# Two block tables and written-out instruction orders in a fused conv-attention, linear-attention and top-2 expert kernel

## The chip, the cores and the metric

One core of one Trainium2 chip runs the whole program. The metric is the device time in microseconds of one execution, the median of the runs. The profiled execution is one of them, with the profiler on.

## The reference

Eight images of 128 channels and 256 pixels go through three stages, each of which adds its result to its input. Tokens are (image, pixel) pairs, 2048 of them.

```python
# stage 1, conv attention, per image: softmax over the pixels of the same image
sim = einsum('bpm,bpn->bmn', q, k) / sqrt(64) + key_mask ; x = x + gamma * softmax(sim) @ v
# stage 2, linear attention over t = layernorm(tokens): the sequence is the image index (L = 8),
# the batch is the pixel, 8 heads of 16; causal: image i reads images j <= i
kv_cum = cumsum(k_ v^T) ; attn = (q_ . kv_cum) / max(q_ . k_cum, 1e-6) ; t = t + attn @ out_w.T + out_b
# stage 3, mixture of 8 experts, top 2 per token, over layernorm(t)
routing_weights, selected = top_k(softmax(x @ router_w), 2) ; renormalised to sum 1
out = sum_e combine[e] * ((silu(x @ w1[e]) * (x @ w3[e])) @ w2[e]) ; t = t + out
```

## The kernel before

**Attention stage.** Each image passes through conv attention (`conv_*`), linear attention (`lin_*`) and routing (`route_*`). The functions of one image are spread over later steps: `run_step(step, (stage, lag), ...)` calls, for each engine on its own, `stage(step - lag)` in the listed order. Engines are strictly in order and meet by semaphores. `lin_scores` (L652) makes, for image i, 2(i+1) products of a 128x128 weight (`qk`) with a moving operand of 8 columns; `lin_products` and `lin_values` are VectorE's large multiplications over i+1 images; `lin_out_turn` (L664) turns and sums on TensorE.

**Routing.** `route_top`, `route_index`, `route_mask`, `route_rank` and `route_slots` give each of a token's two choices a row in `rows_x` in memory: expert e owns the rows from e*CAP on, filled in order. `scatter` (L442, GpSimd, four indirect DMAs for each image) writes the normalised token, its weight and its destination there; `seen_done` counts the running totals per expert, `hm[:, .., 0, :]`.

**Table.** After image 7, TensorE sums the counts (L716), VectorE works out the first row and the expert of each of 39 blocks of 128 rows (L998 to L1014), TensorE turns the result (L718) and VectorE stores it as `table` (L1017). Engines read the table into registers with `table_reader`. `pad_lists` writes one block of empty rows behind each expert's list. SyncE waits for the table, the pads and all 32 scatters, then loads blocks (L395, `xb`, a ring of 12). TensorE runs 16 warm-up matmuls (L752).

**Expert stage.** For each of the 39 blocks: `turn_x` (L724), `gate_up` (L733, 4 f32 matmuls of 128x128, recorded as 8), ScalarE `silu` (L555), VectorE `hidden` (L1023), `down` (L742), VectorE `weigh` (L1040), and a scattered store to `rows_y` by GpSimd (L454). VectorE copies each block's gate and up weights from `W13` to `WB` (L1030), which is a ring of 3.

**End.** When every store has landed, SyncE loads both halves of `rows_y` in 6 parts (L404, L405), VectorE adds them to `t2` (L1058, L1060) and SyncE stores the result (L409).

Of the kernel before, what the change touches and what calls it, by code (L numbers as in the profile page):

```python
# [7 lines left out]
ALU = mybir.AluOpType  # L8
# [7 lines left out]
P = 128  # L16
B = 8
# [5 lines left out]
H = 8  # L23
# [10 lines left out]
BLOCKS = TOP_K * TOKENS // P + E - 1  # L34
ROW = P + 2
# [3 lines left out]
RING = 12  # L39
# [9 lines left out]
WARM_MATMULS = 16  # L49
SPLIT_FROM = 3  # L50
STEPS = B + 12
# [9 lines left out]
C_END = C_TURN_ROW + 1  # L61
# [8 lines left out]
def constants():  # L70
# [10 lines left out]
    f[:, C_TURN_ROW] = np.arange(P) * P  # L81

# [8 lines left out]
def hybrid_block(nc, x_ch, x_tok, w_conv, w_lin, w_router, w13, w2, vecs, bias_rows, cst_f, cst_tri, cst_dest,  # L91
                 out):
    ctx = ExitStack()
    with ctx:
# [15 lines left out]
        W13 = sb("W13", [P, E * 2 * F])  # L110
        W2 = sb("W2", [P, E * FK * P])
# [44 lines left out]
        num = sb("num", [P, 2, B, T * P])  # L156
        attT = sb("attT", [P, 2, N])
# [17 lines left out]
        cnt = sb("cnt", [P, E])  # L175
        pad_row = sb("pad_row", [1, E], I32)
        up = sb("up", [P, E], I32)
        nbi = sb("nbi", [P, E], I32)
        nblk = sb("nblk", [P, E])
        one8 = sb("one8", [P, E])  # L180
        ends = sb("ends", [P, E])
        past = sb("past", [BLOCKS, E])
        skipped = sb("skipped", [BLOCKS, E])
        exp_f = sb("exp_f", [BLOCKS, 1])
        first_f = sb("first_f", [BLOCKS, 1])
        rel_f = sb("rel_f", [BLOCKS, 1])
        row_f = sb("row_f", [BLOCKS, 1])
        steer = sb("steer", [BLOCKS, 2])
        table = sb("table", [2, BLOCKS], I32)
        pad = sb("pad", [P, ROW])  # L190
# [8 lines left out]
        y1 = sb("y1", [P, NT, P])  # L199
        y2 = sb("y2", [P, NT, P])  # L200
# [18 lines left out]
        ps_log = bank(BANK_LOG)[:, 0:T * E].rearrange("p (t e) -> p t e", t=T)  # L219
        ps_rank = bank(BANK_RANK)[:, 0:T * E].rearrange("p (t e) -> p t e", t=T)  # L220
        ps_cnt = bank(7)[:, N + 2 * T * E:N + 2 * T * E + E]

        ps_table = bank(7)[0:2, N + 2 * T * E + E:N + 2 * T * E + E + BLOCKS]
        ps_xbT = [bank(n)[:, 0:P] for n in BANKS_XBT]
        ps_yb = [bank(n)[:, 0:P] for n in BANKS_YB]
        ps_warm = bank(5)[:, 0:2 * P]
# [4 lines left out]
        ld_x = [sem(f"ld_x{i}") for i in range(B)]  # L231
        ld_vec = sem("ld_vec")
# [34 lines left out]
        qk_done = sem("qk_done")  # L267
        sc_done = sem("sc_done")
# [18 lines left out]
        scattered = sem("scattered")  # L287
        cnt_done = sem("cnt_done")
        pad_row_done = sem("pad_row_done")
# [3 lines left out]
        pads_stored = sem("pads_stored")  # L293
# [20 lines left out]
        hid_done = sem("hid_done")  # L314
        wb_done = sem("wb_done")
# [20 lines left out]
        def run_step(step, *stages):  # L336

            for stage, lag, *which in stages:
                if 0 <= step - lag < B:
                    stage(step - lag, *which)  # L340

        def pad_lists(eng, experts):
            eng.wait_ge(pad_row_done, 1)
            held = [eng.alloc_register(f"pad_row{e}") for e in experts]
            eng.reg_load(held, pad_row[0:1, experts[0]:experts[-1] + 1])
            for reg in held:
                row = eng.snap(reg, min_val=0, max_val=DUMMY - P)
                eng.dma_start(rows_x[bass.ds(row, P), :], pad[:, :]).then_inc(pads_stored, 16)

        def table_reader(eng, line, most):  # L350

            sets = [[eng.alloc_register(f"line{line}_{half}_{n}") for n in range(READ)] for half in range(2)]

            def read(s):
                held = sets[s // READ % 2]
                if s % READ == 0:
                    m = min(READ, BLOCKS - s)
                    eng.reg_load(held[0:m], table[line:line + 1, s:s + m])
                return eng.snap(held[s % READ], min_val=0, max_val=most)
            return read  # L360
# [746 lines left out]
```

## Time and profile before

| | us |
|---|---|
| runs: median (lowest to highest) | 214.12 (211.87 to 215.71) |
| profiled execution, device time | 212.14 |
| its span, first to last instruction | 210.3 |
| TensorE busy | 157.1 |
| VectorE busy | 125.7 |
| ScalarE busy | 67.9 |
| GpSimd busy | 83.8 |

The profiled execution spends 212.14 - 210.3 = 1.84 us outside its span. Busy time is a union of instruction intervals; an engine can be 60% busy on average and still be full in one stage. Times below count from the start of the span.

### The profile page before, as it was taken

To read this page: it belongs to the slowest core of one execution; us is meant where nothing else is said; L and a number is where in the kernel's file an instruction comes from. 1 tells how busy PE (TensorE), PEld (TensorE's weight loads), DVE (VectorE), ACT (ScalarE), POOL (GpSimd) and SP (SyncE) were. 2 spreads that over 40 slices of the span, in tenths; PEclk is the share of its full clock that TensorE was granted. 3 is DMA by queue.
4 is the path that set the end of the run, shared out by engine and by line. 5 is a ranking of instruction groups with operands and counts; after the bars stand their busy time and mean duration, and the time that the engine had idled before them with its cause. 6 is when DMAs were issued, how large, how long until landed. Compare 5 with 4: busy or idle time off the path is not lost.

```text
span 210.3 us, 4205 instructions
## 1 busy us (share of the span) xinstructions
PE 157.1 (75%) x1173; PEld 142.4 (68%) x1173; DVE 125.7 (60%) x465; ACT 67.9 (32%) x210; POOL 83.8 (40%) x94
## 2 busy tenths in 40 slices
PE   0999999999989799955340089998899989985000
PEld 0677899999989798944230059998888988884000
DVE  0526778797996879792456202666665655564054
ACT  2267776646442221221013003333333233331000
POOL 0001111202017263767677700665556655557100
PEclk9999999999996969699555556999999999999555
DMA  4889300000001010101113324132223232110296
GB/s 122 240 254 388 147 3 0 3 0 0 5 0 38 16 34 17 41 25 52 40 40 105 98 61 106 42 90 75 68 79 84 70 81 79 47 37 10 76 295 230
DMA packets 15477, 16.81 MB, mean 80 GB/s; under 512 B 3084, under 2 KB 14033, under 8 KB 15199
## 3 DMA queue, kind: packets, MB, share of 16 engines
q1 hardware_dynamic: 12606, 12.05, 19.2%
q0 software_dynamic: 2272, 4.24, 6.4%
q10 hardware_dynamic: 576, 0.27, 0.5%
q8 instruction: 10, 0.16, 0.3%
q14 instruction: 13, 0.10, 0.2%
HBM read 10.66 MB, written 6.33 MB: 81 GB/s over the span
## 4 chain that ended last, share of the span: by engine, by line
PE 64%; issue 9%; DMA 7%; DVE 6%; POOL 4%; another core or an unknown queue 3%; SPq 3%; ACT 2%; POOLq 1%; DVEq 0%
PE ps L733 18%; PE ps L742 8%; PE ps L652 7%; PE ps L593 4%; PE ps L613 4%; POOL rows_x L442 3%; PE ps L637 2%; DMA y<-rows_y 2%; PE ps L724 2%; PE ps L631 2%; PE ps L630 2%; PE ps L603 2%; PE ps L578 2%; DMA rows_x<-xrow,slot 2%
## 5 line engine op out<-in xcount | busy, mean ns | idle before, releaser
L454 POOL DMA_INDIRECT rows_y<-yb,xb x39 | 39.1, 1002 | 36.1 <-DVE yb L1040 28.3
L733 PE MATMUL ps<-xbT,WB 128*128 128x128 f32 x312 | 43.8, 286 | 5.1 <-issue 5.1
L733 PEld LDWEIGHTS ps<-xbT,WB 128*128 128x128 f32 x312 | 39.6, 199 | 7.2 <-issue 7.1
L442 POOL DMA_INDIRECT rows_x<-xrow,slot x32 | 31.9, 996 | 24.5 <-DVE slot L985 16.3
L1040 DVE TENSOR_SCALAR yb<-ps,xb 128x128 f32<-128x128 f32 x39 | 13.6, 349 | 24.4 <-PE ps L742 23.7
L555 ACT ACTIVATE gate<-ps 128x256 f32<-128x256 f32 x39 | 15.0, 386 | 37.7 <-PE ps L733 31.5
L742 PE MATMUL ps<-W,hid 128*128 x156 | 23.8, 277 | 0.5 <-DVE yb L1040 0.5
L426 POOL TENSOR_TENSOR rs<-ve,CF 128x2 f32<-128x2 f32 x8 | 5.6, 700 | 43.7 <-DVE ve L836 43.7
L1023 DVE TENSOR_TENSOR hid<-gate,ps 128x256 f32<-128x256 f32 x39 | 16.2, 414 | 8.7 <-ACT gate L555 8.6
L742 PEld LDWEIGHTS ps<-W,hid 128*128 128x128 f32 x156 | 20.5, 192 | 0.7 <-issue 0.7
L1030 DVE COPY WB<-W 128x512 f32 x39 | 16.5, 427 | 1.4 <-issue 1.3
L652 PEld LDWEIGHTS ps<-CF,qk 128*128 128x128 f32 x144 | 17.0, 194 | 0.1
L549 ACT ACTIVATE xbT<-ps 128x128 f32<-128x128 f32 x39 | 10.9, 280 | 18.7 <-PE ps L724 16.8
L652 PE MATMUL ps<-CF,qk 128*128 128x8 f32 x144 | 16.9, 253 | 0.0
L854 DVE TENSOR_TENSOR qk<-kT,qT 128x768 f32<-128x768 f32 (+3 forms) x13 | 11.6, 891 | 2.7 <-ACT kT L509 1.5
L892 DVE TENSOR_TENSOR num<-vt,sco 128x768 f32<-128x768 f32 (+3 forms) x13 | 11.5, 893 | 1.2 <-ACT vt L513 1.0
L724 PE MATMUL ps<-CF,xb 128*128 128x128 f32 x39 | 11.2, 287 | 0.4 <-DMA xb<-rows_x 0.4
L664 PE MATMUL ps<-CF,num 128*128 128x128 f32 x72 | 10.1, 289 | 0.0
L578 PE MATMUL ps<-X,WC 128*65 128x256 f32 x16 | 5.8, 452 | 5.1 <-DMA XT<-in_x_tok 5.1
L593 PE MATMUL ps<-ck,cq 65*128 65x256 f32 x32 | 9.3, 417 | 0.1
L688 PEld LDWEIGHTS ps<-WR,x2T 128*128 128x128 f32 x32 | 5.1, 224 | 5.9 <-issue 5.8
L688 PE MATMUL ps<-WR,x2T 128*128 128x8 f32 x32 | 5.3, 274 | 5.1 <-DVE where L976 4.7
(122 smaller groups left out, 284.7 us busy)
## 6 DMA issues: line engine op xcount, KB each, us to landing
xb<-rows_x SPq DMA_DIRECT2D x39, 65.0 KB
W<-in_w SPq DMA_DIRECT2D x1, 2048.0 KB, 10.3
y<-rows_y SPq DMA_DIRECT2D x8, 192.0 KB, 4.4
X<-in_x_ch SPq DMA_DIRECT2D x8, 128.0 KB, 3.0
XT<-in_x_tok SPq DMA_DIRECT2D x8, 128.0 KB, 3.5
W<-in_w SPq DMA_DIRECT2D x1, 1024.0 KB, 12.9
out_tok<-y SPq DMA_DIRECT2D x4, 192.0 KB, 3.0
rows_y<-yb,xb POOLq DMA_INDIRECT x39
```

The lines of the kernel that those rows point to most:

```text
L442: pool.indirect_dma_start(rows_x, bass.IndirectOffsetOnAxis(ap=slot[:, g:g + 1], axis=0), xrow[:, i * T + t, c, :], None, bounds_check=DUM ...
L454: pool.indirect_dma_start(rows_y, bass.IndirectOffsetOnAxis(ap=xb[:, n, DEST_COL:ROW].bitcast(I32), axis=0), yb[:, n, :], None, bounds_che ...
L555: act.activation(gate[:, s % GATE, :], ps_gu[s % 3][:, 0:F], ACT.Silu).then_inc(gate_done, 1)
L593: last = pe.matmul(ps_sim[:, t, :], cq[:, b, t * P:(t + 1) * P], ck[:, b, :], start=True, stop=True)
L652: last = pe.matmul(ps_sc[:, j, t * H:(t + 1) * H], qk[:, i % 2, j, t * P:(t + 1) * P], heads, start=True, stop=True)
L724: pe.transpose(ps_xbT[s % 2], xb[:, s % RING, 0:P], ident).then_inc(xbT_done, 1)
L733: last = pe.matmul(ps_gu[s % 3][:, k * P:(k + 1) * P], WB[:, s % WBS, k * P:(k + 1) * P], xbT[:, s % XBT, :], start=True, stop=True)
L742: last = pe.matmul(ps_yb[s % 2], hid[:, s % HID, k * P:(k + 1) * P], W2[:, bass.ds(e * (FK * P) + k * P, P)], start=(k == 0), stop=(k == F ...
L854: dv.tensor_tensor(qk[:, i % 2, first:end, :], kT[:, first:end, :], qT[:, i % 2, :].unsqueeze(1).broadcast_to([P, end - first, N]), ALU.mult)\
L1023: dv.tensor_tensor(hid[:, s % HID, :], gate[:, s % GATE, :], ps_gu[s % 3][:, F:2 * F], ALU.mult)\
L1030: dv.tensor_copy(WB[:, s % WBS, :], W13[:, bass.ds(experts[s] * (2 * F), 2 * F)]).then_inc(wb_done, 1)
L1040: dv.tensor_scalar(yb[:, n, :], ps_yb[s % 2], xb[:, n, W_COL:W_COL + 1], None, ALU.mult).then_inc(yb_done, 1)
```

## The change

- **Two tables.** `PHASES = ((5, 13), (8, 39))`: a first table is made when five images are routed and names 13 blocks, all of them full ones (`is_ge` counts whole blocks; 5 images are 2560 rows, at most 7 of whose 20 blocks' worth can be lost to unfilled blocks of 8 experts). A second table is made after image 7 for the other 26. `scattered` becomes a semaphore for each phase.
- **Orders written out.** The `run_step` loops are replaced on every engine by one list of calls, in which blocks 0 to 12 stand among the routing of images 5 to 7.
- **Wide head sums.** `lin_scores` multiplies by 128 columns of `HZ`, which is zero but for 8 of them, and sums all products of an image into one accumulation. `HZ` is filled by GpSimd at the start.
- **Blank rows.** `pad_lists` and its waits go. Instead all of `rows_x` is blanked early from `W13`'s space (8 DMAs, 128 x 2210 f32 each, and one of 128 x 130), and only then are `W13` and `W2` loaded. The scatter of image 0 waits for the blanking.
- **Weight copies.** For blocks 0 to 12, ScalarE copies `W13` to `WB`; for the rest VectorE does, as before.
- **Loads.** SyncE loads block s once TensorE has turned block s - 5 (`LOOK`); the ring grows from 12 to 16.
- **Start.** Conv weights and `VEC` are loaded from ScalarE's queue, the other copy of image 0 has its own semaphore, and 22 small matmuls run first; the 16 warm-up matmuls before the expert stage go.
- Image 3 and later use another bank for logits and ranks. `y1` and `y2` lie in `num`.

The diff, cut to what is spoken of:

```diff
+PHASES = ((5, 13), (B, BLOCKS),)
+LAST = len(PHASES) - 1
+SPANS = [(0 if p == 0 else PHASES[p - 1][1], PHASES[p][1]) for p in range(len(PHASES))]
-RING = 12
+RING = 16
+LOOK = 5
...
 SyncE
-            sp.dma_start(WC[:, :], w_conv).then_inc(ld_conv, 16)
-            sp.dma_start(VEC[:, :], vecs).then_inc(ld_vec, 16)
...
+            sp.wait_ge(pad_ready, 2)
+            for e in range(E):
+                sp.dma_start(rows_x[e * CAP:(e + 1) * CAP, :].rearrange("(p k) d -> p k d", p=P), pad[:, :, :])\
+                  .then_inc(rows_blank, 16)
...
+            sp.wait_ge(rows_blank, 16 * (E + 1))
             sp.dma_start(W13[:, :], w13).then_inc(ld_w13, 16)
             sp.dma_start(W2[:, :], w2).then_inc(ld_w13, 16)
...
+            for p, (first, last) in enumerate(SPANS):
+                row = first_row(first)
+                sp.wait_ge(scattered[p], 16 * T * TOP_K * images_of(p))
+                for s in range(first, last):
+                    if s - first >= LOOK:
+                        sp.wait_ge(xbT_done, s - LOOK + 1)
...
 GpSimd
+            scatter(3, 3); scatter(4, 0); scatter(4, 1); scatter(4, 2); scatter(4, 3); rstd_ffn(5); rstd_ffn(6)
+            scatter(5, 0); rstd_ffn(7); scatter(5, 1); scatter(5, 2); store(0); scatter(5, 3); scatter(6, 0)
+            scatter(6, 1); scatter(6, 2); scatter(6, 3); scatter(7, 0); scatter(7, 1); scatter(7, 2); scatter(7, 3)
+            for s in range(1, BLOCKS):
+                store(s)
...
 ScalarE
+                act.activation(WB[:, s % WBS, :], W13[:, bass.ds(experts[s] * (2 * F), 2 * F)], ACT.Copy)\
+                   .then_inc(wb_early, 1)
...
+            lin_xT(7); lin_v(7); lin_qk(7); route_lean(4); lin_aT(5); weights(0); weights(1); lin_aT(6); route_xT(5)
+            lin_aT(7); turned_x(0); weights(2); turned_x(1); route_lean(5); silu(0); weights(3); turned_x(2)
...
 TensorE
                 for j in range(first, end):
-                    heads = CF[:, C_COS + (i - j) * H:C_COS + (i - j + 1) * H]
                     for t in range(T):
-                        last = pe.matmul(ps_sc[:, j, t * H:(t + 1) * H], qk[:, i % 2, j, t * P:(t + 1) * P], heads,
-                                         start=True, stop=True)
+                        at = (B * T - 1 - (j * T + t)) * H
+                        last = pe.matmul(ps_sc, qk[:, i % 2, j, t * P:(t + 1) * P], HZ[:, i - j, at:at + B * T * H],
+                                         start=(j == 0 and t == 0), stop=(j == i and t == T - 1), skip_group_check=True)
...
+            lin_scores(6, 0); lin_scores(6, 1); lin_out_turn(5, 0); route_rank(4); count(0); lin_out_turn(5, 1)
+            lin_out(5); lin_scores(7, 0); lin_scores(7, 1); lin_out_turn(6, 0); t_turn(0); lin_out_turn(6, 1)
+            route_turn(5); lin_out(6); route_logits(5); lin_out_turn(7, 0); lin_out_turn(7, 1); turn_x(0)
+            lin_out(7); turn_x(1); gate_up(0); route_rank(5); route_turn(6); turn_x(2); gate_up(1); turn_x(3)
+            gate_up(2); down(0); route_logits(6); turn_x(4); gate_up(3); down(1); turn_x(5); gate_up(4); down(2)
...
+            gate_up(12); down(10); down(11); down(12); turn_x(13); turn_x(14); gate_up(13); turn_x(15); gate_up(14)
+            for s in range(14, BLOCKS + 1):
+                block_step(s)
...
 VectorE
+            def t_blocks(p):
+
+                steps = CF[:, C_STEP:C_STEP + STEPS_OF_ROWS] if p == LAST else CF[:, C_STEP + 1:C_END]
+                dv.wait_ge(cnt_done, p + 1)
+                dv.tensor_tensor(tall[:, p, :, :], ps_cnt[p].unsqueeze(2).broadcast_to([P, E, STEPS_OF_ROWS]),
+                                 steps.unsqueeze(1).broadcast_to([P, E, STEPS_OF_ROWS]),
+                                 ALU.is_gt if p == LAST else ALU.is_ge).then_inc(tall_done, 1)
+
+            def t_sum(p):
+                dv.wait_ge(tall_done, p + 1)
+                dv.tensor_reduce(nblk[:, p, :], tall[:, p, :, :], AX.X, ALU.add).then_inc(nblk_done, 1)
...
+            lin_sum(6); lin_products(7, 1); t_blocks(0); route_where(4); lin_floor(6); t_sum(0); route_slots(4)
+            lin_inverse(6); t_ends(0); t_delta(0); lin_weights(6); t_past(0); lin_add(5); t_skip(0); t_expert(0)
+            route_stats(5); t_row(0); lin_values(6, 0); route_moments(5); lin_values(6, 1); route_eps(5); t_done(0)
+            lin_sum(7); lin_floor(7); t_read(0); lin_inverse(7); lin_weights(7); route_norm(5); lin_values(7, 0)
+            lin_add(6); lin_values(7, 1); route_stats(6); route_top(5); route_moments(6); route_index(5)
...
+            weigh(11); weigh(12); weights(13); weights(14); weights(15); hidden(13); weights(16); hidden(14)
```

The order on TensorE between the last rank of the attention stage and the first block's turn, before: the count, the table's turn, the warm-up, then blocks.

```order
L705 MATMUL ps<-hm,TRI 128x16
L716 MATMUL ps<-hm,TRI 128x8
L718 MATMUL ps<-CF,steer 2x39
L752 MATMUL ps<-TRI 128x256 x16
L358 TENSOR_LOAD table
L724 MATMUL ps<-CF,xb 128x128 x2
L733 MATMUL ps<-xbT,WB 128x128 x4
L724 MATMUL ps<-CF,xb 128x128
```

After: the end of the attention stage, from the output projection of image 6 (L762, L763) on; `x2T` is image 5's.

```order
L763 MATMUL ps<-BIAS,ONES 128x128
L762 MATMUL ps<-WL,attT 128x128
L763 MATMUL ps<-BIAS,ONES 128x128
L777 MATMUL ps<-WR,x2T 128x8 x2
L752 MATMUL ps<-CF,num 128x128 x16
L814 MATMUL ps<-CF,xb 128x128
L762 MATMUL ps<-WL,attT 128x128
L763 MATMUL ps<-BIAS,ONES 128x128
L762 MATMUL ps<-WL,attT 128x128
L763 MATMUL ps<-BIAS,ONES 128x128
L814 MATMUL ps<-CF,xb 128x128
```

The logits of image 5 and the last turn of image 7 stand directly ahead of the first block's turn, and the output projection of image 7 stands behind it.

ScalarE at the same place, before: the four pad stores, then the blocks.

```order
L347 ISA
L348 DMA rows_x<-pad 128x130
L347 ISA
L348 DMA rows_x<-pad 128x130
L549 ACTIVATE xbT<-ps 128x128 x2
L555 ACTIVATE gate<-ps 128x256
L549 ACTIVATE xbT<-ps 128x128
```

After:

```order
L390 TENSOR_LOAD table0
L391 ISA
L614 ACTIVATE WB<-W13 128x512
L391 ISA
L614 ACTIVATE WB<-W13 128x512
L571 ACTIVATE attT<-ps 128x256
L577 ACTIVATE x2T<-ps 128x256
L571 ACTIVATE attT<-ps 128x256
L596 ACTIVATE xbT<-ps 128x128
L391 ISA
L614 ACTIVATE WB<-W13 128x512
```

The table's read and two weight copies now stand between the attention output of image 5 (`attT`) and that of image 6.

GpSimd's last rows, before: all scatters (L442), then 39 stores (L454).

```order
L442 DMA rows_x<-xrow,slot 17536x130 x4
L432 TENSOR_TENSOR rs2<-ve2,CF 128x2
L442 DMA rows_x<-xrow,slot 17536x130 x4
L432 TENSOR_TENSOR rs2<-ve2,CF 128x2
L442 DMA rows_x<-xrow,slot 17536x130 x12
L454 DMA rows_y<-yb,xb 4096x128 x39
```

After (L485 scatters, L472 `rstd_ffn`, L494 stores):

```order
L485 DMA rows_x<-xrow,slot 17536x130 x8
L472 TENSOR_TENSOR rs2<-ve2,CF 128x2 x2
L485 DMA rows_x<-xrow,slot 17536x130
L472 TENSOR_TENSOR rs2<-ve2,CF 128x2
L485 DMA rows_x<-xrow,slot 17536x130 x2
L494 DMA rows_y<-yb,xb 4096x128
L485 DMA rows_x<-xrow,slot 17536x130 x9
L494 DMA rows_y<-yb,xb 4096x128 x38
```

One store stands among the twelve scatters of images 5 to 7, and 38 behind them.

## Rows read from the trace of the kernel before

**Rows 1.** The page, span in 40 slices: TensorE and VectorE busy, TensorE's granted clock.

```profile
PE   0999999999989799955340089998899989985000
...
DVE  0526778797996879792456202666665655564054
...
PEclk9999999999996969699555556999999999999555
```

**Rows 2.** Windows: window, length, busy (count) of PE, PEld, DVE, ACT, POOL, then PEclk, DMA share, GB/s.

```profile
10.00:20.00 10.00, 9.44 (x51) 7.32 (x50) 4.39 (x14) 6.23 (x18) 0.72 (x1) 1.00 0.89 308
...
125.00:135.00 10.00, 9.70 (x66) 9.39 (x67) 4.21 (x13) 3.64 (x12) 2.37 (x2) 0.76 0.34 81
135.00:155.00 20.00, 18.56 (x161) 17.84 (x160) 12.53 (x38) 6.74 (x24) 12.12 (x12) 1.00 0.30 79
```

**Rows 3.** Timeline, first matmul: start, length, engine, line, tiles, what it waited for.

```profile
5.13 1.09 PE L578 MATMUL ps<-X,WC 128*65 128x256 f32 x2 [5.13 <-DMA XT<-in_x_tok]
```

**Rows 4.** Windows of 5 us in the attention stage, same columns as Rows 2.

```profile
65.00:70.00 5.00, 4.63 (x28) 3.91 (x27) 2.78 (x18) 1.94 (x5) 4.05 (x5) 0.67 0.16 53
...
85.00:90.00 5.00, 5.00 (x37) 4.72 (x36) 3.54 (x16) 0.77 (x2) 4.07 (x5) 0.66 0.13 43
```

**Rows 5.** Timeline: two logits of TensorE, image 2's and image 5's.

```profile
70.92 0.58 PE L688 MATMUL ps<-WR,x2T 128*128 128x8 f32 x4 [1.29 <-DVE where L976]
...
95.84 0.51 PE L688 MATMUL ps<-WR,x2T 128*128 128x8 f32 x4
```

**Rows 6.** The chain of work that ended last: start, length, what.

```profile
56.85 0.45 PE ps L631 x2
...
66.32 0.85 PE ps L631 x2
...
81.97 3.53 PE ps L652 x32
...
119.41 3.65 DMA rows_x<-xrow,slot
123.83 1.90 DMA xb<-rows_x
...
186.19 0.89 PE ps L733 x8
...
194.68 2.08 DMA rows_y<-yb,xb
```

**Rows 7.** Timeline from the count to the first block's turn.

```profile
112.07 0.17 PE L716 MATMUL ps<-hm,TRI 128*128 128x8 bf16 x1 [0.59 <-issue]
...
118.41 0.19 DVE L1017 CAST table<-ps 2x39 int32<-2x39 f32 x1 [1.51 <-issue]
...
119.91 1.10 DVE L1030 COPY WB<-W 128x512 f32 x3 [1.31 <-issue]
...
125.14 0.47 PE L724 MATMUL ps<-CF,xb 128*128 128x128 f32 x1 [0.29 <-DMA xb<-rows_x]
```

**Rows 8.** Timeline of GpSimd.

```profile
63.24 1.19 POOL L442 DMA_INDIRECT rows_x<-xrow,slot  x1 [4.46 <-DVE slot L985]
...
89.51 1.33 POOL L432 TENSOR_TENSOR rs<-ve,CF 128x2 f32<-128x2 f32 x1
...
180.78 0.98 POOL L454 DMA_INDIRECT rows_y<-yb,xb  x1 [0.30 <-issue]
```

**Rows 9.** Timeline of TensorE in the expert stage.

```profile
179.47 1.13 PE L733 MATMUL ps<-xbT,WB 128*128 128x128 f32 x8 [0.49 <-issue]
...
184.50 1.13 PE L733 MATMUL ps<-xbT,WB 128*128 128x128 f32 x8 [0.45 <-issue]
...
192.08 0.71 PE L742 MATMUL ps<-W,hid 128*128 x4 [0.52 <-DVE yb L1040]
```

**Rows 10.** Groups by line: count, busy us, mean ns, idle: copies of 128x512.

```profile
L1030 DVE COPY WB<-W 128x512 f32 x39 | 16.5, 427 | 1.4 <-issue 1.3
...
L496 ACT ACTIVATE probT<-ps 128x512 f32<-128x512 f32 x8 | 4.8, 601 | 1.3 <-PE ps L603 1.2
```

More of the change, by code:

```diff
@@ L173, in hybrid_block @@
         slot = sb("slot", [P, NT * TOP_K], I32)
[L175 to L179, printed above, removed]
-        one8 = sb("one8", [P, E])
[L181 to L190, printed above, removed]
+        tall = sb("tall", [P, len(PHASES), E, STEPS_OF_ROWS])
+        one8 = sb("one8", [P, E])
+        nblk = sb("nblk", [P, len(PHASES), E])
+        csum = sb("csum", [P, len(PHASES), E])
+        ends = sb("ends", [P, len(PHASES), E])
+        done = sb("done", [P, len(PHASES), E + 1])
+        taken = sb("taken", [P, len(PHASES), E])
+        ahead = sb("ahead", [P, len(PHASES), E])
+        turn = sb("turn", [P, len(PHASES), 1])
+        delta = sb("delta", [P, len(PHASES), E])
+        past = sb("past", [BLOCKS, len(PHASES), E])
+        skip = sb("skip", [BLOCKS, len(PHASES), E])
+        exp_f = sb("exp_f", [BLOCKS, len(PHASES)])
+        row_f = sb("row_f", [BLOCKS, len(PHASES)])
+        steer = sb("steer", [BLOCKS, len(PHASES), 2])
+        table = [sb(f"table{p}", [2, last - first], I32) for p, (first, last) in enumerate(SPANS)]
         xb = sb("xb", [P, RING, ROW])
@@ L563, in _ @@
+            weights(11); turned_x(10); silu(9); weights(12); turned_x(11); silu(10); turned_x(12); silu(11)
+            silu(12); turned_x(13)
+            for s in range(12, 38):
+                turn_and_silu(s)
         @block.tensor
@@ L571, in bank_free, with warm_up @@
                 bank_users[bank_number] = (read, count)
+            def warm_up():
+                pe.wait_ge(dve, 1)
+                for _ in range(22):
+                    pe.matmul(ps_aT[:, 0:P], ONES[:, :], ONES[:, :], start=True, stop=True)
             def conv_proj_qk(i):
@@ L744, in down, with block_step @@
                 last.then_inc(yb_done_pe, 1)
-            pe.wait_ge(ld_w13, 32)
-            pe.wait_ge(table_done, 1)
-            pe.wait_ge(pads_stored, 16 * (E + 1))
-            for _ in range(WARM_MATMULS):
-                pe.matmul(ps_warm, TRI[:, 0:P], TRI[:, :], start=True, stop=True)
-            expert = table_reader(pe, T_EXPERT, E - 1)
-            experts = [expert(0)]
-            for s in range(-2, BLOCKS + 1):
+            def block_step(s):
                 if s + 2 < BLOCKS:
@@ L779, in _ @@
             link(dv.memset(ECB[:, :], 0.0))
+            dv.memset(done[:, :, E:E + 1], float(2 * BLOCKS))
             dv.memset(one8[:, :], 1.0)
```

454 lines of the change are left out of this document (302 added, 152 removed).

## The prediction, made before the change was run

> **What bounds the kernel now.** I read the page's slices first [rows 1], then the chain of waits [rows 6], then timelines around the places where an engine stands still. The slices show three parts. From slice 2 to 17 TensorE is 9 to 10 tenths busy and VectorE 7 to 9: the attention stage, with both engines nearly full. Slices 18 to 23 are a trough: TensorE at 0 to 5 tenths, and its clock at 0.5, the lower of the two levels. Then come the expert blocks at 9 tenths, and an end without TensorE.
>
> Four marks cut the span. The first matmul starts at 5.13 [rows 3]. The last thing that TensorE does before the trough is the logits of image 5, at 95.84 to 96.35 [rows 5]; by then all conv and linear attention is through, but for one output projection. The first block is turned at 125.14 [rows 7], and the last `down` ends at 192.08 + 0.71 = 192.79 [rows 9]. So: start 5.1, attention 91.2, trough 28.8, blocks 67.7, end 17.5, together 210.3. The trough is a chain of latencies: routing of images 5 to 7, GpSimd's scatters one after the other until 119.41, the landing of the last (3.65), the first block's load (1.90) [rows 6]. Hardly any of it is TensorE's work, which is what the change exploits: it needs something to put there, and the blocks are it.
>
> **Start.** Image 0's projections wait for the fifth transfer on SyncE's queue, `XT`, which they do not read [rows 3]. After the change they need `X`, first on that queue, and the conv weights, first on ScalarE's. Two issues are 0.47 us apart, so three issues less give -1.4 (bounds -0.5 and -2). Later steps of image 0 (its maximum, its exponentials) have their own latency and are not touched.
>
> **Wide head sums.** 32 records of 8 columns took 3.53 us in the chain, 0.110 each; 8 records of 128 columns took 0.89, 0.111 each [rows 6]. A wide product should thus cost what a narrow one does: 0 for the 72 of them. Against this stands the Trainium skill, page "TensorE: Matmul & The Clock Gate", section "Step-by-step: what each phase is for", where the streaming phase takes as many cycles as the moving operand has columns. By that rule alone 8 columns would be almost free and 72 wide products would add some 72 x 0.22 = 16 us. The rows do not agree with it for the narrow ones, which are as slow as wide ones here.
>
> What can change is the clock. It is 1.00 until 60 us, then 0.67 and 0.66 in the windows from 65 and from 85 [rows 4] and 0.66 in one from 75, each right behind one of the three longest narrow bursts (24, 28 and 32 records). A projection of 256 columns takes 0.85 there and 0.45 at the full clock [rows 6]. Work lost: 5 x (0.33 + 0.34 + 0.34) = 5.0 us. If the wide sums keep 2.4 GHz through the burst, that is -5.0; if not, 0. I take -5.0, since the falls come only behind those bursts.
>
> **Order of the attention stage.** The list of calls ahead of the first block's turn holds the same matmuls as the stage up to 96.35, so that mark can be moved: 96.35 - 1.4 - 5.0 = 90.0. TensorE has six idle stretches between 59 and 94, ahead of logits, ranks, turns and a projection; the longest is 1.29 [rows 5], the shortest 0.30, together 4.7 us. Another order can save half, -2.4. But VectorE, at 7 to 9 tenths, has the same work, and has to finish image 4's routing before it; two engines that are both this full seldom fit together without gaps: +2.0 (bounds 0 and +7).
>
> **The first table.** After `count(0)` VectorE has about 35 instructions up to the table, among them the value products of image 6 at some 2 us, in all 7.4 us; before, 6.34 passed from the count to the table (112.07 to 118.41) [rows 7]. A table read costs 1.3 (118.60 to 119.91) [rows 7]. On ScalarE two weight copies of about 0.60 each [rows 10] follow the read, and behind them is queued `lin_aT(6)`, for which TensorE's `lin_out(6)` waits; then VectorE's addition for image 6, half of the value products of image 7 (1.1), and their turn. I get 13.6 us from `count(0)` to the first block's turn, where the matmuls in between fill 9.2: +4.4 (bounds +2 and +9). The block's rows take the other way round: four scatters of image 4 at 1.28, 3.65 + 1.9 for landing and load, about 12 us from the count, so they are just hidden. First turn: 90.0 - 2.4 + 2.0 + 4.4 = 94.
>
> **Blocks.** Three blocks take 5.03 us (179.47 to 184.50, two others between) [rows 9], 1.68 each, with one short stop of TensorE in each three. That loop is unchanged from block 14 on. Terms on top of the 67.65: the lower clock of the first 10 us goes (0.76 [rows 2], -2.4), if TensorE comes in warm; matmuls of routing and `lin_out(7)` now stand among blocks, +3.4 (three ranks at 0.3, two turns at 0.2, two logits at 0.6, a projection at 0.65, the count and the second table's turn at 0.2 together); VectorE's routing among the first ten blocks costs some 14 us of work against 20 of TensorE there, so it is hidden but for shared moments, +2. At the second table, `down(12)`, `weigh(12)`, VectorE's table read (1.3) and its first copy (0.43 [rows 10]) stand in series before `gate_up(13)`, which nothing hides since the order drains the blocks there: +2.4 (up to +8 if the last scatter is late). Blocks: 67.65 - 2.4 + 3.4 + 2 + 2.4 = 73.05.
>
> **GpSimd.** It keeps a step of 1.28 per indirect DMA, 0.98 and a pause of 0.30 [rows 8]. Scatters of images 5 to 7 and store 0 run among the early blocks; the last scatter starts about 21 us after the first turn, so block 13 can be loaded by 27, when TensorE comes to it (13 x 1.68 + 3.4 + the stop). Scatters end near 22; 38 stores take 49 from there, until 71; the last block is through at 73. GpSimd is two microseconds short of being the bound, and the ring of 16 gives room.
>
> **Hidden.** Blanking is 8 x 128 x 2210 x 4 bytes = 9.05 MB. At the 263 GB/s that 79 GB/s at a share of 0.30 imply for short packets [rows 2] it takes 34 us, at 308/0.89 = 346 it takes 26; started near 12 us it ends by 38 to 46, and the 3 MB of weights by 60. The first scatter came at 63.24 [rows 8], will come near 60, and the first weight copy near 88: cover of 14 and of 28 us. `LOOK` of 5 blocks is 8 us against a load of 1.9 [rows 6]. The ScalarE copy costs no time there: copy, turn and gate together 1.3 of 1.68.
>
> **Sum.** 94 + 73.05 + 17.5 = 184.5 span, with the 1.84 outside it 186.4. The profiled execution is 2 us below the median of the runs, so I name 187.
>
> **Rivals.** (a) *GpSimd becomes the bound.* The Trainium skill, page "SBUF — State Buffer", section "SBUF: two separate sides", says that a VectorE copy of f32 locks GpSimd out of writing descriptors. By it the 26 copies of 0.43 left on VectorE add 11 us to the stores. Here a store at 180.78 beside a copy took 0.98 [rows 8], as most do, so the trace disagrees; but one small GpSimd operation took 1.33 beside large products, and GpSimd now works beside VectorE throughout. With 0.25 more for each of 50 steps: +12 less 2 of slack, 197. Chance 0.10. (b) *VectorE bounds the attention stage* or the first table takes its upper end: first turn at 101, 194. Chance 0.12. (c) *The overlap is not had*: the second table's scatters come late, so that 13 blocks are done early but TensorE stands for 8 to 12 us before block 13: 195 to 199. Chance 0.08. (d) *Slower than before*: the blanking. Scatter 0 waits for it, and twenty scatters with the powers between them (33 us) and the landing must pass before a block. It decides from about 85 us on, when the first turn comes at 123 and the total at 216; that needs 9.05 MB to run at under 124 GB/s. A mean of 308 in 10 to 20 us [rows 2] speaks against it. Chance 0.02. (e) Better than the forecast: no loss to VectorE, start and order at their good ends, 176 to 180. Chance 0.10. The forecast, 181 to 193, has 0.58.
>
> **Range and chances.** 179 to 198 leaves out (d), the worst of (a) and (c), the best of (e): about 0.15. What a measurement can tell from no change is 2%, 4.3 us. Faster by over 2%: 0.96; within: 0.02; slower: 0.02.
>
> **What the profile after should show.** Clock 1.00 through the bursts of head sums; the first block's turn at 92 to 97 with scatters of images 5 to 7 behind it; no trough, but a stop of some 4 us ahead of the first block and of 2 to 4 ahead of block 13; blocks 14 on at 1.68; blanking over before 46; GpSimd without pause after block 12. Wrong would be: an attention stage that ends past 101, blocks 0 to 12 at over 2 us, or stores that end more than 4 us after the last `down`.

## The result, and the profile after

| | before | after |
|---|---|---|
| median of the runs, us | 213.5 (211.87 to 215.71, 4 runs) | 201.94 (200.66 to 204.29, 4 runs) |
| ratio to before | 1 | 0.946, 95% interval 0.936 to 0.956 |
| the profiled execution: time, span | 212.14, 210.3 | 201.57, 199.4 |

The change gains 5.4%, where 187 (179 to 198) was predicted: the sign is right, more than half of the gain (11.6 us of 26.5) is missing, and the time lies outside the range. Medians are of all executions of a run; some kernels have a second group of longer times, and ratios compare the shorter group alone.

The slices of the page after, to be read against [rows 1] (the same three, and GpSimd):

```profile
PE   7979999998999899969976880547999899991000
DVE  0646678886979898955735530034566666642154
...
POOL 8001112148814854631373477743366656666000
PEclk9999999999999999996997999555899999999555
```

The clock holds through the head sums (slices 9 to 17), and the trough of before is filled. But there is a new hole in slices 23 to 26, with TensorE at 8, 8, 0, 5 tenths, VectorE at 0, 0, 3 and only GpSimd at 7. The marks of the prediction, in timelines of TensorE: the first block's turn, the turns of blocks 13 and 14 (one row), the last `down`.

```profile
93.19 0.27 PE L814 MATMUL ps<-CF,xb 128*128 128x128 f32 x1
...
134.16 0.63 PE L814 MATMUL ps<-CF,xb 128*128 128x128 f32 x2
...
180.81 0.71 PE L839 MATMUL ps<-W,hid 128*128 x4 [1.10 <-DVE hid L1205]
```

So: first turn 93.2 (predicted 94), blocks 0 to 12 take 41.0 us, the others to the last `down` (181.52) 47.4, the end 17.9. Against the predicted 94 + 73.05 + 17.5 the blocks are 15.3 us long, most of it in the first thirteen, and the rest agrees within 1 us.

The chain of waits, where [rows 6] had scatters and the block's load, has pieces between 101 and 132 us that no work of an engine fills:

```profile
101.66 3.68 another core or an unknown queue
...
117.02 4.25 another core or an unknown queue
...
121.32 2.85 another core or an unknown queue
...
124.22 6.97 another core or an unknown queue
```

That is 17.8 us, more than the whole miss (14.9). What stands there, the timeline of all engines (start, length, engine, line, operation, tiles; in brackets the idle time before and its releaser; "remote" is a releaser that the profile could not name, as in the chain):

```profile
116.15 1.06 PE L828 MATMUL ps<-xbT,WB 128*128 128x128 f32 x8
...
117.05 0.61 PE L839 MATMUL ps<-W,hid 128*128 x4
...
118.01 0.97 POOL L485 DMA_INDIRECT rows_x<-xrow,slot  x1 [0.30 <-issue]
...
119.29 0.97 POOL L494 DMA_INDIRECT rows_y<-yb,xb  x1 [0.30 <-issue]
...
120.56 0.97 POOL L494 DMA_INDIRECT rows_y<-yb,xb  x1 [0.30 <-issue]
121.30 0.38 ACT L602 ACTIVATE gate<-ps 128x256 f32<-128x256 f32 x1 [4.02 <-remote]
...
124.16 0.35 DVE L1226 TENSOR_SCALAR yb<-ps,xb 128x128 f32<-128x128 f32 x1 [7.42 <-remote]
...
128.22 0.97 POOL L494 DMA_INDIRECT rows_y<-yb,xb  x1 [0.30 <-issue]
131.22 0.66 ACT L602 ACTIVATE gate<-ps 128x256 f32<-128x256 f32 x2 [6.74 <-remote]
```

TensorE's records say that `gate_up(10)` ended at 117.2 and `down(8)` at 117.7. Yet ScalarE gets its gate at 121.30 and VectorE its block at 124.16: the stop lies between TensorE's record and the arrival of its signal. From 114.2 to 129.2 us, around that time, GpSimd issues 4 scatters and 8 stores at a step of 1.28, 0.97 each and 0.30 between two. Late blocks have a small form of the same, and so had those of before [rows 9]: three at full speed, then a stop, with three stores beside them.

```profile
163.94 1.23 POOL L494 DMA_INDIRECT rows_y<-yb,xb  x1 [0.47 <-issue]
...
164.16 1.06 PE L828 MATMUL ps<-xbT,WB 128*128 128x128 f32 x8
...
165.58 0.38 ACT L602 ACTIVATE gate<-ps 128x256 f32<-128x256 f32 x1 [1.95 <-PE ps L828]
...
166.23 1.13 PE L828 MATMUL ps<-xbT,WB 128*128 128x128 f32 x8 [0.46 <-issue]
```

Theory A: GpSimd's indirect DMAs, one behind the other, hold TensorE up. Theory B, the rival: the stops belong to the handover between the tables, or to the refilling of TensorE's instructions (one instruction packet landed near 116), and the stores only happen to be there.

### The profile page after: what moved, and what is told of

Read it like the earlier page. It is cut to its first block, busy times and chain, and to the rows that moved or that the text cites. A ratio compares the mean times of both kernels' runs of the same rounds, so it can differ in the third digit from the quotient of the medians.

```text
span 199.4 us, 4199 instructions
## 1 busy us (share of the span) xinstructions
PE 155.3 (78%) x1181; PEld 142.0 (71%) x1181; DVE 117.7 (59%) x464; ACT 73.2 (37%) x223; POOL 89.4 (45%) x96
## 4 chain that ended last, share of the span: by engine, by line
PE 49%; issue 16%; another core or an unknown queue 9%; POOL 6%; DMA 6%; DVE 5%; ACT 4%; SPq 2%; POOLq 1%; ACTq 1%; DVEq 0%
PE ps L828 17%; PE ps L839 8%; POOL rows_x L485 4%; PE ps L739 3%; PE ps L752 3%; DMA num<-rows_y 3%; PE ps L814 3%; PE ps L698 2%; PE ps L678 2%; DMA BR<-in_bias_rows 2%; PE ps L715 1%; PE ps L716 1%; PE ps L722 1%; PE ps L688 1%
## 5 line engine op out<-in xcount | busy, mean ns | idle before, releaser
L828 PE MATMUL ps<-xbT,WB 128*128 128x128 f32 x312 | 46.1, 295 | 8.8 <-issue 8.5
L494 POOL DMA_INDIRECT rows_y<-yb,xb x39 | 39.7, 1019 | 26.5 <-DVE yb L1226 17.1
L828 PEld LDWEIGHTS ps<-xbT,WB 128*128 128x128 f32 x312 | 41.8, 208 | 11.0 <-issue 11.0
L485 POOL DMA_INDIRECT rows_x<-xrow,slot x32 | 33.8, 1056 | 25.8 <-DVE slot L1107 18.0
L839 PE MATMUL ps<-W,hid 128*128 x156 | 26.0, 296 | 5.9 <-DVE hid L1205 5.9
L602 ACT ACTIVATE gate<-ps 128x256 f32<-128x256 f32 x39 | 14.9, 385 | 42.7 <-PE ps L828 28.2
L739 PE MATMUL ps<-HZ,qk 128*128 128x128 f32 x144 | 18.2, 277 | 0.4 <-DVE sco L996 0.4
L739 PEld LDWEIGHTS ps<-HZ,qk 128*128 128x128 f32 x144 | 17.2, 192 | 0.9 <-issue 0.6
L472 POOL TENSOR_TENSOR rs<-ve,CF 128x2 f32<-128x2 f32 x8 | 5.7, 708 | 20.0 <-DVE ve L1037 19.8
L466 POOL TENSOR_TENSOR rs<-ve,CF 128x2 f32<-128x2 f32 x8 | 5.8, 729 | 19.4 <-DVE ve L955 19.4
L752 PE MATMUL ps<-CF,num 128*128 128x128 f32 x72 | 11.7, 307 | 0.0
L1216 DVE COPY WB<-W 128x512 f32 x26 | 11.0, 430 | 0.8 <-issue 0.8
L614 ACT ACTIVATE WB<-W 128x512 f32 x13 | 8.0, 625 | 7.9 <-issue 7.8
L752 PEld LDWEIGHTS ps<-CF,num 128*128 128x128 f32 x72 | 9.7, 161 | 0.4
L541 ACT ACTIVATE prob<-ps,nmax 128x256 f32<-128x256 f32 x16 | 7.4, 469 | 6.0 <-DVE nmax L921 6.0
```

The costliest lines, as they stand in the source:

```text
L485: pool.indirect_dma_start(rows_x, bass.IndirectOffsetOnAxis(ap=slot[:, g:g + 1], axis=0), xrow[:, g // TOP_K, g % TOP_K, :], None, bounds_ ...
L494: pool.indirect_dma_start(rows_y, bass.IndirectOffsetOnAxis(ap=xb[:, n, DEST_COL:ROW].bitcast(I32), axis=0), yb[:, n, :], None, bounds_che ...
L602: act.activation(gate[:, s % GATE, :], ps_gu[s % 3][:, 0:F], ACT.Silu).then_inc(gate_done, 1)
L739: last = pe.matmul(ps_sc, qk[:, i % 2, j, t * P:(t + 1) * P], HZ[:, i - j, at:at + B * T * H], start=(j == 0 and t == 0), stop=(j == i and ...
L752: last = pe.matmul(ps_aT[:, t * P:(t + 1) * P], num[:, i % 2, j, t * P:(t + 1) * P], ident, start=(j == 0 and t == 0), stop=(j == i), is_t ...
L828: last = pe.matmul(ps_gu[s % 3][:, k * P:(k + 1) * P], WB[:, s % WBS, k * P:(k + 1) * P], xbT[:, s % XBT, :], start=True, stop=True)
```

## Experiments

Each is the changed kernel with the edit shown, or the one before where it says so. "Before" is the kernel before on the same chip in the same series.

| run | edit | us | before |
|---|---|---|---|
| e1_plain_stores | stores plain | 181.45 | 214.42 |
| e2_no_early_stores | stores 1 to 12 out | 194.76 | 214.42 |
| e3_spaced | pauses, 512 columns | 210.17 | 214.42 |
| e4_late_stores | stores 1 to 12 held back | 205.37 | 214.42 |
| e5_pause128 | pauses, 128 columns | 205.32 | 212.04 |
| e6_pause1 | pauses, 1 column | 207.32 | 212.04 |
| e7_narrow | narrow head sums | 212.79 (205.21 to 215.88) | 212.04 |
| b1_before_plain | before, stores plain | 203.99 | 212.04 |
| b2_before_wide | before, wide head sums | 211.80 | 211.60 |
| b3_before_wide_plain | both | 202.79 | 211.60 |
| e8_filler | e4 and 120 free matmuls | 214.70 | 211.60 |
| c1_sooner_stores | stores 0 to 3 sooner | 203.62 | 211.60 |
| e9_skipped | stores that move no row | 206.54 | 211.32 |
| e10_pause256 | pauses, 256 columns | 201.98 | 211.32 |
| e11_pause_all | 256 columns, among scatters too; stores 0 to 3 sooner | 206.28 | 211.32 |
| after_again | none | 206.55 (202.14 to 207.64) | 211.32 |
| c2_pause_until33 | e10, none for the last 6 | 197.18 | 211.94 |
| after_third | none | 201.81 | 211.94 |

### Take the indirect stores away

```diff
-                pool.indirect_dma_start(rows_y, ...ap=xb[:, n, DEST_COL:ROW]..., yb[:, n, :], ...)
+                pool.dma_start(rows_y[s * P:(s + 1) * P, :], yb[:, n, :])
```

> GpSimd stores each finished block with a plain DMA to the block's own place instead of an indirect DMA to the tokens' rows; the bytes are the same, the order of the rows in the output is not. Theory A (while GpSimd issues indirect DMAs one behind the other, 0.97 us each at a step of 1.28, the signals that TensorE sends at the end of its matmuls arrive late): without the 39 stores only the scatters hold signals back. The stop from 118 to 131 us shrinks to about 3 us (-9), and the stop of 1.8 us in every third block of the last 25 goes, if not wholly (-5): about 187 us. Theory B (the stops come from the order at the handover between the tables, or from TensorE's instruction refills, and the stores are bystanders): 200 to 202 us, stops at the same places.

Measured: 181.45, ratio to before 0.865 (0.849 to 0.880): 20 us below the changed kernel's 201.94. GpSimd and TensorE in the timeline of late blocks:

```profile
140.50 0.54 POOL L493 DMA_DIRECT2D rows_y<-yb  x1 [0.91 <-DVE yb L1223]
141.95 0.54 POOL L493 DMA_DIRECT2D rows_y<-yb  x1 [0.91 <-DVE yb L1223]
...
141.21 1.06 PE L825 MATMUL ps<-xbT,WB 128*128 128x128 f32 x8
...
142.66 1.06 PE L825 MATMUL ps<-xbT,WB 128*128 128x128 f32 x8
...
144.11 1.06 PE L825 MATMUL ps<-xbT,WB 128*128 128x128 f32 x8
```

A block takes 1.45 us, each after the other, against 1.68. During ten plain stores in a row (116.83 to 122.17) ScalarE gets the gates of blocks 10, 11 and 12, at 117.26, 117.70 and 119.08; the first is late (its product's record ends at 114.5), with the second right behind it, and there the last scatters run until 116.3. Theory B is out. The gain is larger than A's estimate in both parts: blocks 0 to 12 take 28.8 us instead of 41.0 (A: 9 less), the others 40.6 instead of 47.4 (A: 5 less). Part of that is probably the low clock behind the stop, which goes too (1.00 in 113 to 150 us, against 0.77).

```diff
-            for s in range(1, BLOCKS):
+            for s in range(1, SPANS[LAST][0]):      # blocks 1 to 12: a mark instead of a store
+                pool.wait_ge(yb_done, s + 1)
+                pool.memset(mark[:, s:s + 1], 0.0).then_inc(marked, 1)
+            for s in range(SPANS[LAST][0], BLOCKS):
                 store(s)
```

> The stores of blocks 1 to 12 are left out (GpSimd sets a mark with a memset of one column in their place; the rows of the output that they carry are wrong, and are filled beforehand by two plain DMAs of 1 MB each behind the blanking); the 27 others stay indirect. Theory A: what lies behind the last scatter at 119 us is no longer held back: block 13 starts about 9 us sooner, the last 25 blocks keep their 1.7 us each: 191 to 194 us. Theory B: block 13 starts as before at 134, 200 to 202 us.

Measured: 194.76, where A said 191 to 194 and B 200 to 202; block 13 is turned 31.3 us after block 0, where the changed kernel takes 41.0.

```diff
+            pool.wait_ge(xbT_done, SPANS[LAST][0] + 1)      # block 13 is turned
             for s in range(1, BLOCKS):
                 store(s)
```

> Full computation. GpSimd holds stores 1 to 12 back until the first transpose of the second table (block 13) has ended. Theory A: nothing runs on GpSimd behind the last scatter at 119 us, so the first table's blocks end and block 13 is turned by about 124; then 12 stores stand in a row of 15 us, TensorE's signals come late in that stretch, and part of the loss comes back there: 194 to 202 us, with the late signals moved to 124 to 145. Theory B: the stop from 118 to 131 us stays, and the backlog comes on top: 203 us or more.

Measured: 205.37. By its time alone this is B's range (203 or more); the trace decides for A. The stop from 118 to 131 us, which B keeps, is gone: block 13 is turned at 127.1, 31.6 us behind block 0. The stop moved behind it, and it costs more than A's estimate. Then come 12 stores from 127.6 to 142.9, and ScalarE's gates in the timeline wait for them:

```profile
131.92 0.39 ACT L603 ACTIVATE gate<-ps 128x256 f32<-128x256 f32 x1 [1.21 <-PE ps L829]
...
141.39 0.38 ACT L603 ACTIVATE gate<-ps 128x256 f32<-128x256 f32 x1 [8.46 <-remote]
```

TensorE's record of the second one's product ends at 132.2: 9.2 us between record and signal.

### What is held: the signals, or TensorE?

```diff
 turn_x(13); turn_x(14); gate_up(13); turn_x(15); gate_up(14)        (on e4_late_stores)
+            pe.wait_ge(x2T_read, B)
+            pe.wait_ge(table_done, 2)
+            for _ in range(120):
+                pe.matmul(bank(7)[:, 0:P], ONES[:, :], ONES[:, :], start=True, stop=True)
```

> On the kernel that holds 12 stores back: 120 matmuls of 128 columns, on constants, into an unused bank, with nothing to wait for, stand in TensorE's order behind gate_up(14), where GpSimd's run of 12 stores begins. If only TensorE's signals are held while GpSimd issues indirect DMAs, the 120 matmuls run on at 0.06 or 0.11 us each through the run (7 to 13 us). If TensorE itself is held, their records show a hole of several us, until the run ends, and the time grows by the 7 to 13 us on top of 205: 212 or more. In the first case the time grows less, since TensorE would have stood there anyway: 205 to 208.

Measured: 214.7, 9 us over e4 (two executions, another chip). The windows of those matmuls alone (window, length, busy (count) of PE, PEld, then clock, DMA share, GB/s), GpSimd's run being 126.1 to 141.3:

```profile
129.50:131.30 1.80, 1.79 (x33) 1.79 (x33) 1.00 0.40 109
131.30:143.20 11.90, 4.14 (x26) 1.90 (x23) 0.58 0.20 62
143.20:150.10 6.90, 6.87 (x65) 6.85 (x65) 0.50 0.00 0
```

33 are taken at 0.055 each, then 22 until 143.2 us (the window counts 26, since records that cross its start stand in both), then, the run being over, 65 at 0.106. Both waits ahead of them were met long before, so TensorE itself is held, not only its signals. It wasn't waiting for instructions to be loaded by DMA either: one instruction packet comes between 130 and 131 us and none from 131 to 150, while 87 of these matmuls start. The first 33 I read as those that it takes ahead into a queue, which would also make records look early and signals late; that is argued, not shown.

### Is it GpSimd's work, or the rows that it moves?

```diff
-  rows_y, bass.IndirectOffsetOnAxis(ap=xb[:, n, DEST_COL:ROW].bitcast(I32), axis=0),
+  rows_y, bass.IndirectOffsetOnAxis(ap=nowhere[:, :], axis=0),      # SKIP on every partition
```

> The changed kernel with its 39 indirect stores given an index beyond the bound on every partition: GpSimd issues them as before, but no row is moved (rows_y is filled beforehand by two plain DMAs, the output is not the reference's). If it is GpSimd's own work on an indirect DMA that stops TensorE, the stops stay: 198 to 203 us. If it is the transfers (the small writes to the rows in the chip's memory), they go, as with plain stores: 181 to 185 us.

Measured: 206.54 (205.51 to 207.00). The changed kernel beside it has a median of 206.55, but over 202.14 to 207.64, so the times don't settle it; they exclude the 181 to 185 of the other theory. The trace does: blocks 0 to 12 take 40.7 us (41.0 in the changed kernel) and the others 48.1 (47.4), with the same stops. ScalarE's gates of blocks 10, 11 and 12:

```profile
125.55 0.38 ACT L610 ACTIVATE gate<-ps 128x256 f32<-128x256 f32 x1 [4.08 <-remote]
135.64 0.66 ACT L610 ACTIVATE gate<-ps 128x256 f32<-128x256 f32 x2 [3.37 <-PE ps L836]
```

The page's line of the software queue, of this run, of the changed kernel, and of e1 with its plain stores (packets, MB, share):

```profile
q0 software_dynamic: 2272, 2.15, 3.6%
```

```profile
q0 software_dynamic: 2272, 4.24, 6.4%
```

```profile
q0 software_dynamic: 2272, 4.69, 7.7%
```

In e9 the bytes of the stores are gone, the packets (now empty) and GpSimd's 0.97 us an instruction are not, and the stop is whole. In e1 bytes and packets are there, as many packets as before, and the stop is gone. So it is neither the rows nor the packets, but what GpSimd does to issue an indirect DMA. The Trainium skill, page "DMA: Bandwidth & Descriptors", section "SWDGE vs HWDGE vs iDMA", has GpSimd's cores write each such DMA's descriptors into rings in SBUF before anything moves. That section of the Trainium skill says so of GpSimd's plain and indirect DMAs alike, and the plain ones of e1 held nothing up, so it doesn't give the reason. No run here shows these rings, nor by which path the work reaches TensorE.

### How far apart must they be?

```diff
             for s in range(1, BLOCKS):
+                pool.memset(mark[:, :], 0.0).then_inc(paused, 1)     # 1, 128, 256 or 512 columns
+                pool.wait_ge(paused, s)
                 store(s)
```

> Full computation. GpSimd runs a memset of 512 columns (about 0.45 us by the 1.93 us of 2193 columns) and waits for it ahead of every store from the second on, so that stores follow each other at about 1.9 us instead of 1.28. Theory A: TensorE's signals pass in the pauses, none is over 1.5 us late; the first table's part gains 5 us or more, but 25 stores at 1.9 us (47 us against 42) bound the last part: 197 to 203 us, and the pattern of three blocks gives way to one block at a time. Theory B: GpSimd only gets slower, the stops at 101 and 117 to 131 us stay: 206 us or more.

> Full computation; as the run with pauses of 512 columns, but with memsets of 128 columns (about 0.27 us with its wait, by 0.60 us for 512), so that stores follow each other at about 1.55 us. Theory A (TensorE's signals wait for a gap in GpSimd's run of indirect DMAs, and a pause of this size is enough): TensorE goes through the last 25 blocks at 1.44 to 1.55 us each, the backlog of 12 stores at block 13 is worked off slowly (0.1 us a block) and costs little: 193 to 197 us. Rival: the pause has to be longer than this; the pattern of three blocks stays, and the pauses only lengthen it: 203 to 208 us.

> As before with memsets of one column (about 0.1 us and a wait), stores at about 1.4 us. Theory A with a short gap being enough: 190 to 195 us. Theory A with a gap of some 0.5 us being needed: the three-block pattern stays at 5.1 us or more, 201 to 204 us.

> Full computation, pauses of 256 columns ahead of stores 1 to 38 (steps of about 1.6 us; at 1.45 TensorE was still stopped, at 1.8 no longer). If 1.6 is enough: TensorE keeps 1.44 us a block, the stores end at 119.3 + 38 x 1.6 = 180, 198 to 200 us. If not: the pattern of three blocks stays and is longer, 205 to 208.

Measured: 210.17, 205.32, 207.32, 201.98. With 1 and 128 columns stores stand 1.36 and 1.47 apart and the pattern of three blocks stays: the rival was right, though with one column the time is 3 us above its range. With 512, TensorE goes through a block each 1.45 us, as A said, but stores stand 1.8 to 2.0 apart and end at 193, which I had priced too low: the time is in B's range, the pattern is A's. With 256 they stand 1.57 apart right behind the scatters, where TensorE is still slowed (gates 10 to 12 at 126.3, 130.1, 132.3), and mostly 1.57 to 1.7 from 143 us on, where most blocks take 1.45. Its time is level with the shorter executions of the changed kernel in all three series (201.94, 202.14, 201.81), so this run shows the mechanism and no gain; its 201.98 lies between the two ranges that were expected. The change of behaviour lies between 1.47 and some 1.6 us; at 1.57 both occur.

> Full computation, the same pauses ahead of the scatters from image 5's second on too, and stores 0 and 1 ahead of image 6's scatters, 2 and 3 ahead of image 7's. If 1.6 us between indirect DMAs is enough for TensorE to run on: the first 13 blocks take about 30 us instead of 41, GpSimd is the only bound: 51 indirect DMAs from 97 us at 1.6 us is 179, with 3 us of idle time 182, and 17 behind: 195 to 199 us. If not: 205 to 210.

Measured: 206.28, in the second range, yet the trace shows the first one's mechanism. ScalarE's gates of blocks 0 and 12, timeline:

```profile
98.79 0.38 ACT L618 ACTIVATE gate<-ps 128x256 f32<-128x256 f32 x1 [0.43 <-PE ps L844]
...
117.86 0.38 ACT L618 ACTIVATE gate<-ps 128x256 f32<-128x256 f32 x1 [0.96 <-PE ps L844]
```

Twelve blocks in 19.1 us. In the changed kernel gate 0 is at 95.75 and gate 12 at 131.6, 35.8; with plain stores 24.3. By these differences the scatters take some 5 and the stores 11 (an estimate: e11 also has four stores at other places). But the last scatter starts at 131.1 instead of 118.0 (a pause and a wait made it 2.1 us a scatter), and the second table waits for it.

> Full computation. Stores 0 and 1 go ahead of image 6's scatters and stores 2 and 3 ahead of image 7's, into time in which GpSimd waits for slots (104.5 to 107.2, 112.0 to 114.2 us), so that 9 instead of 12 stores stand behind the last scatter. Theory A: the run from 114 to 129 us gets 3 stores shorter (-3.8), some of it lost again since the pauses in which TensorE's signals passed are filled: 198 to 202 us. Rival (the length of the run doesn't matter): 202 or more.

Measured: 203.62, the rival's time. What the trace shows is not that the length of the run is nothing, but that the gaps between the scatter groups were TensorE's. Filled, they put image 7's first scatter 25 us behind the first block's turn instead of 21.

```diff
             for s in range(1, BLOCKS):
-                pause()
+                if s < 33:
+                    pause()
                 store(s)
```

> Full computation: pauses of 256 columns ahead of stores 1 to 32, none ahead of the last 6, which in the run with pauses throughout stood behind TensorE's last blocks (store 33 at 176 us, the last block's multiply at 177.5). If pauses cost only where nobody is stopped, this is 2 us (6 x 0.37) below the run with all pauses, 199 to 201 us, and 3 to 6 us below the changed kernel on the same chip. If the gain of the pauses was chance, it is within 1.5 us of the changed kernel.

> The changed kernel beside it on the same chip, to settle whether the pauses gain: 201 to 207 us, as in the two series so far (201.9 and 206.6).

> The changed kernel as it is, beside these on the same chip: 200 to 204 us.

Measured: 197.18 (195.80 to 197.72), against 201.81 (200.28 to 202.80) beside it on the same chip (the 206.55 of the series before lies above the 200 to 204 that were expected of it). No run of the one reaches into the other's. The computation is whole, so this is the best version here: 0.941 of before (0.933 to 0.950), 2.3% below the changed kernel. That is the 3 to 6 us below it that were expected, but 2 us under the expected 199 to 201. Its timeline at 142 us shows the mechanism:

```profile
142.43 1.05 POOL L504 DMA_INDIRECT rows_y<-yb,xb  x1 [0.28 <-POOL mark L498]
143.48 0.33 POOL L498 MEMSET mark<- 128x256 f32 x1
144.08 1.04 POOL L504 DMA_INDIRECT rows_y<-yb,xb  x1 [0.28 <-POOL mark L498]
...
142.25 1.06 PE L840 MATMUL ps<-xbT,WB 128*128 128x128 f32 x8
...
143.70 1.06 PE L840 MATMUL ps<-xbT,WB 128*128 128x128 f32 x8
```

From 134 to 150 us GpSimd is busy for 13.5 of 16 us, with stores and memsets, and TensorE for all 16: a busy GpSimd by itself holds nothing up. The stores set the end now: TensorE's last `down` ends at 171.4, 10 us sooner than in the changed kernel, but the last store is only issued at 178.1 (183.0 there).

### What the parts of the change are worth

```diff
-  pe.matmul(ps_sc, qk[...], HZ[:, i - j, at:at + B * T * H], ...)
+  pe.matmul(ps_sc[:, j, t * H:(t + 1) * H], qk[...], CF[:, C_COS + (i - j) * H:...], ...)
```

> The changed kernel with the head sums in their narrow form again (8 columns a matmul, each into its own columns of the bank); all else, the memset of the wide table too, stays. By the prediction's clock term: the granted clock falls to 0.5 to 0.75 in slices between 40 and 80 us, as in the kernel before, and the first block's turn comes 5 us later: 206 to 207 us. Rival (the term was not there; VectorE sets the pace of the attention at either clock): within 1 us of the changed kernel, 201 to 203.

Measured: 212.79. Nine of ten executions lie at 212 or more, one at 205.21, and the changed kernel was not run on this chip. Against its 201.94 the wide sums are worth about 11 us by the nine, and 3 by the one, where 5 or nothing was expected; why one is so short is open. The profiled execution is one of the nine. The timeline of TensorE at image 6's burst and at the first turn, narrow, and then the burst in the changed kernel:

```profile
77.61 5.98 PE L738 MATMUL ps<-CF,qk 128*128 128x8 f32 x28
...
102.82 0.27 PE L813 MATMUL ps<-CF,xb 128*128 128x128 f32 x1
```

```profile
74.15 3.29 PE L739 MATMUL ps<-HZ,qk 128*128 128x128 f32 x28
```

The granted clock is 0.71 in 60 to 80 and 0.52 in 80 to 100 us. Where the clock is at its lower level, a narrow record takes 0.21, so the burst itself doubles, which I had not counted: I had only the fall behind bursts that ran at the high level.

> The kernel before, with the wide head sums alone (and the final sum's buffers laid over those of the attention values to make room): one table, stores indirect. If the wide sums are worth what the run with narrow ones showed (11 us), this is 201 to 203 us, and the two tables and the rest of the change together gave nothing with indirect stores. If they are worth the 5 us of the prediction, 207, and the rest gave the other 5.

> The kernel before with plain stores (each block to its own place, rows of the output in another order). Theory A: the stops of 1.8 us in every third block go, 34 blocks at 1.45 instead of 1.69 us: 205 to 207 us, 24 to 26 above the changed kernel with plain stores (181.5), which is what the prediction summed for the change (27) without the held signals. Theory B: 213 us.

> The same with plain stores (rows of the output in another order). Theory A: the overlap of the first 13 blocks with the attention is worth what the prediction said (about 15 to 20 us of the whole) as long as no signal is held: 193 to 197 us here against 181.5 of the changed kernel with plain stores. Rival (the overlap is worth nothing by itself): 182 to 184 here.

Measured: 211.80 (ratio 1.001, 0.997 to 1.005), 203.99 (200.64 to 206.09), 202.79. Only the second comes near what was expected: b2 lies above both of its ranges, and so does b3, by 6 us or more. The wide sums by themselves give nothing: in b2 GpSimd's last 12 scatters stand in one run from 107.5 to 122.6, and the first block is turned at 126.7, no sooner than before (105.3 to 120.5, and 125.1). The two tables with narrow sums give nothing either in nine of ten executions (e7). Together they give about 11. With plain stores the change is worth some 21 us (202.79 or 203.99 to 181.45, on three chips), and by b3 nearly all of it is not in the wide sums by themselves.

## Why the prediction was wrong, point by point

- **Start, order, first table**: first turn at 93.2 for 94 (94.8 and 96.4 in the two repetitions). Right in sum, in part by luck, for the sum hides an error in one term: **the wide sums** were worth not 5.0 but 6 to 10 by the first turn (102.8 in e7's profiled execution), so order, VectorE and table together cost some 1 to 4 more than I gave them. The mechanism, that the clock stays at its upper level through the bursts, was right: it is 1.00 from 60 to 86 us, where e7 has 0.71 in 60 to 80 and 0.52 in 80 to 100.
- **Blocks**: the step that failed. "GpSimd is two microseconds short of being the bound, and the ring of 16 gives room" took GpSimd's 1.28 per DMA as work beside TensorE's. It is work in TensorE's place: in runs of indirect DMAs TensorE is held (e8). "With one short stop of TensorE in each three" stood in my own text [rows 9], as part of a loop that goes on unchanged; its cause was not asked for. That stop is 0.24 us a block where stores come in threes (1.68 against 1.45), and 10 to 12 us over the first thirteen blocks, where twelve indirect DMAs stand in a row (41.0 against 31.3 in e2 and 28.8 in e1). Of the prediction's three signs of being wrong, this one came: blocks 0 to 12 at 3.2 us each.
- **The handover**: +2.4, "up to +8 if the last scatter is late". The last scatter started 24.8 us behind the first turn (118.0), where I had 21, but that cost nothing: TensorE came to block 13 only at 134.2, and its row there shows no wait. Rival (c) comes nearest with 195 to 199, still 3 us short, and had nearly the picture, but named the wrong cause; TensorE stood at blocks 10 to 12, whose rows had long been loaded and turned.
- **Rival (a)**: GpSimd did set the time, but by holding TensorE, not through a lock by VectorE's copies: most of its stores keep 0.97 us beside them, some take 1.11 to 1.23, and their mean is 1.02 (1.00 before). The chance of 0.10 was low for an engine whose stores are in step with the only irregular thing in TensorE's loop.
- **Blanking**: hidden, as said: the weights' loads behind it are issued at 37.1, and the first scatter comes at 42.2 us, not near 60. Rival (d) is out, and so are (b), whose first turn was 101, and (e). **LOOK** was not varied.
- **The pace of 1.68** was right from 150 to 180 us. Before it stands a stretch at a low clock behind the stop (0.78 in 134 to 150 us), and the last 26 blocks take 47.4 us, where 26/39 of 67.65 is 45.1. **The end** was right (17.9 for 17.5).
- **The forecast** is 187, but the sum gives 186.4 for a profiled execution that was said to be 2 us below the median: by that reading it should have been 188.4. It changes nothing here.
- **Narrow against wide products**: that one costs as much as the other held (28 records in 3.29 us wide). Every record, narrow or wide, has a weight load of 128 x 128 beside it (0.19 us in both, rows of L738 in e7 and of L739), which the prediction's argument from columns leaves out; no run separates the two.
- With the stops gone, the prediction's sum comes nearer: e1 has its first turn at 92.3 and a change worth some 21 us, where 27 was summed.

## What to carry to other kernels

A short stop that comes back in every third turn of a loop has a cause, and the cause can grow when the change lets work gather; ask for it before counting the loop as fixed. Indirect DMAs from GpSimd are not free company for TensorE: spread them (here to a step of 1.6 us or more), and leave them dense where TensorE has nothing to do. A gain can need two parts: here the wide sums alone were worth nothing (b2), and the tables without them nothing in nine of ten executions (e7).

## What of the hardware was not expected

GpSimd's indirect DMAs at a step of 1.28 (0.97 each) held TensorE: 22 free matmuls in 11.7 us, against 0.055 us each before (e8). At 1.36 and 1.47 the stops stayed (e6, e5); at 1.57 some blocks were still slowed and most not (e10); at 1.8 to 2.0 they were gone (e3). Plain DMAs from GpSimd, ten in 5.34 us, did not do it (e1), and indirect ones that moved no row did (e9). A matmul's record ended 9.2 us ahead of its signal in e4. What the two engines share is open.
